# Preparing the next feed-forward batch one group sooner, with all weight sums on VectorE

## The reference

```python
def ternary_quant(w):
    scale = jnp.mean(jnp.abs(w)) + EPS
    q = jnp.clip(jnp.round(w / scale), -1.0, 1.0) * scale
    return w + jax.lax.stop_gradient(q - w)
...
up = jnp.einsum('bsd,ed->bse', x, wu)        # 512 -> 2048
gate = jnp.einsum('bsd,ed->bse', x, wg)      # 512 -> 2048
hidden = jax.nn.silu(up) * gate
return jnp.einsum('bse,de->bsd', hidden, wd) # 2048 -> 512
```

## Time and profile before

| | |
|---|---|
| Median of 3 runs | 760.04 us (760.04 to 761.48) |
| The profiled execution: its own time, and its span from first to last instruction | 760.04 us, 758.1 us |
| Busy share of the span: TensorE matmul, VectorE, ScalarE, GpSimd | 92%, 66%, 39%, 33% |
| TensorE clock granted, mean, as a share of 2.4 GHz | 0.973 |
| First product of the feed-forward part | 404.58 us |

### The profile page before, as it was taken

How to read it: one execution, slowest core, us unless ns; L and a number is a source line. 1 busy time by engine, 2 the same in 40 slices (tenths; PEclk the granted TensorE clock), 3 DMA queues, 4 the chain that set the end, 5 groups by cost and what they waited for, 6 DMA issues and landing times.

```text
span 758.1 us, 12681 instructions
## 1 busy us (share of the span) xinstructions
PE 695.5 (92%) x4745; PEld 457.6 (60%) x4776; DVE 503.4 (66%) x814; ACT 295.2 (39%) x450; POOL 250.6 (33%) x242
## 2 busy tenths in 40 slices
PE   7999999999998799999889999499977999499995
PEld 5565456556564656665447777377755777377772
DVE  5566766766757565567756978388773978457664
ACT  4365554554545244443322433234332343123330
POOL 4204523333334600003640343435431543414222
PEclk9999999999999999999999999899997999899998
DMA  8924035036046587601220030202111120201001
GB/s 246 338 81 142 1 128 206 0 125 208 1 155 234 166 326 253 243 29 42 50 50 1 1 51 1 49 1 81 25 26 25 52 54 1 50 1 56 1 1 55
DMA packets 57910, 67.37 MB, mean 89 GB/s; under 512 B 35072, under 2 KB 35072, under 8 KB 56832
## 3 DMA queue, kind: packets, MB, share of 16 engines
q1 hardware_dynamic: 54016, 54.03, 23.5%
q0 software_dynamic: 3840, 12.59, 4.4%
HBM read 46.69 MB, written 12.59 MB: 78 GB/s over the span
## 4 chain that ended last, share of the span: by engine, by line
PE 74%; DVE 9%; issue 7%; ACT 4%; DMA 2%; SPq 1%; POOL 1%; another core or an unknown queue 0%; POOLq 0%; DVEq 0%; ACTq 0%
PE bank L1211 26%; PE bank L1482 25%; PE bank L1491 13%; PE bank L1204 4%; PE bank L1404 2%; DVE region L829 2%; PE bank L1368 2%; PE bank L1382 2%; DMA w_att<-stage 2%; DVE late L825 1%; DMA stage<-in_L_attn_Wv_dram 1%; ACT stage L639 1%; ACT stage L519 1%; DVE region L833 1%; ACT tmp L527 1%
## 5 line engine op out<-in xcount | busy, mean ns | idle before, releaser
L1482 PE MATMUL bank<-w_att,region 128*128 128x256 f16 x1024 | 130.9, 277 | 28.5 <-issue 28.5
L1482 PEld LDWEIGHTS bank<-w_att,region 128*128 128x128 bf16 x1024 | 101.6, 99 | 48.7 <-issue 29.9
L1491 PE MATMUL bank<-region,w_moe 128*128 128x512 bf16 x481 | 115.5, 383 | 3.9 <-DVE w_moe L1122 2.1
L1132 DVE TENSOR_TENSOR n<-bank,n 128x512 f32<-128x512 f32 x112 | 71.7, 685 | 55.8 <-PE bank L1482 54.2
L1211 PE MATMUL bank<-late,w_att 128*128 128x512 f16 x384 | 86.8, 382 | 2.0 <-DVE region L872 1.9
L445 POOL TENSOR_TENSOR w_moe<-tmp,w_moe 128x512 f16<-128x512 f32 x30 | 36.0, 1200 | 154.3 <-ACT w_moe L669 154.3
L1491 PEld LDWEIGHTS bank<-region,w_moe 128*128 128x128 f16 x512 | 50.5, 99 | 51.2 <-DVE w_moe L1122 2.6
L326 POOL TENSOR_SCALAR ve<-mv 128x1 f32<-128x1 f32 (+2 forms) x29 | 10.9, 377 | 198.4 <-DVE mv L709 198.3
L662 ACT ACTIVATE n<-n,qs 128x512 f32<-128x512 f32 x64 | 44.5, 718 | 71.8 <-DVE n L1132 71.3
L1482 PE MATMUL bank<-w_att,late 128*128 128x256 f16 x512 | 68.6, 279 | 0.0
L1211 PEld LDWEIGHTS bank<-late,w_att 128*128 128x128 f16 x384 | 37.4, 98 | 45.0 <-DVE region L872 2.7
(11 more groups left out here) (161 smaller groups left out, 1143.1 us busy)
## 6 DMA issues: line engine op xcount, KB each, us to landing
stage<-in_L_ffn_W_up_dram SPq DMA_DIRECT2D x8, 1024.0 KB
stage<-in_L_ffn_W_gate_dram SPq DMA_DIRECT2D x8, 1024.0 KB, 5.4
rows<-sorted_residual SPq DMA_DIRECT2D x4, 1026.0 KB, 8.6
stage<-in_ctx_dram SPq DMA_DIRECT2D x4, 1024.0 KB, 6.6
stage<-in_L_ffn_W_down_dram SPq DMA_DIRECT2D x4, 1024.0 KB
nrm<-in_L_ffn_W_down_dram SPq DMA_DIRECT2D x4, 1024.0 KB, 8.0
n<-sorted_tokens SPq DMA_DIRECT2D x16, 256.0 KB, 5.8
rows<-in_x_dram SPq DMA_DIRECT2D x1, 3072.0 KB, 18.6
```

The lines of the kernel that those rows point to most:

```text
L1132: dve.tensor_tensor(out, wk_ps[(14 * n + m) % 4][:, :], other, ALU.add).then_inc(s["up_add"], 1)
L1482: mm = pe.matmul(wk_ps[bank][:, q * H:(q + 1) * H], w[:, c + q, k * P:(k + 1) * P], x3S_part[slot][:, h, m, k], start=(h == 0 and k == 0), ...
L1491: mm = pe.matmul(ffy_ps[t][:, :], hid[:, u, h, q, (t % 2) * P:(t % 2 + 1) * P], tern[2][:, c + q], start=(begins and q == 0 and h == 0), s ...
```

## The change

For batches 1 to 3 the preparation moves one group sooner. Normalise, sums, `x3_hi` and `x3_lo` of k = 2b+2 now stand in t = 0, those of k = 2b+3 in t = 2; statistics and rsqrt of k = 2b+3 in t = 1, and those of k = 2b+4 in t = 3. Those of k = 2 stand in expert step 15. All eight weight sums are on VectorE, in expert steps 10, 11, 13, 16 and 17 (before: VectorE's four in steps 10, 12, 15 and 16). In the last group only, `downs_before(2)` stands behind the gate products and not between them.

```diff
--- before.py
+++ after.py
@@ -428,11 +428,6 @@
                 pool.wait_ge(s["x3_lo_in"], 16 * k)
             pool.tensor_tensor(x3h[:, 1], x3_flat[:, 0:7 * H], x3h[:, 0], ALU.subtract).then_inc(s["x3_lo"], 1)
 
-        def gate_sum(dst, a, b, op, n):
-            if n > 0:
-                pool.wait_ge(s["gate_sums"], n)
-            pool.tensor_tensor(dst, a, b, op).then_inc(s["gate_sums"], 1)
-
         def send_out(b):
             for t in range(T):
                 pool.wait_ge(s["out_made"], T * b + t + 1)
@@ -447,13 +442,9 @@
 
         third_rsqrt(0)
         third_rsqrt(1)
-        pool.wait_ge(s["unit_copy"], 12 * T)
-        gate_sum(S1[1], A21[1], A22[1], ALU.add, 0)
         x3_lo(0)
-        gate_sum(S3[1], A11[1], A21[1], ALU.subtract, 1)
-        gate_sum(S2[1], S1[1], A11[1], ALU.subtract, 2)
         x3_lo(1)
-        gate_sum(S4[1], A12[1], S2[1], ALU.subtract, 3)
+        third_rsqrt(2)
 
         def group(b, t):
             n = T * b + t
@@ -461,9 +452,9 @@
                 hid_lo(n, 0, 0, g11)
                 hid_lo(n, 1, 3, g22)
             if b + 1 < B and t % 2 == 0:
-                third_rsqrt(2 * b + 2 + t // 2)
-            if b + 1 < B and t % 2 == 1:
                 x3_lo(2 * b + 2 + t // 2)
+            if (b + 1 < B and t == 1) or (b + 2 < B and t == 3):
+                third_rsqrt(2 * b + 3 + t // 2)
             if n < NT - 1:
                 hid_lo(n, 2, 1, g21)
                 hid_lo(n, 3, 2, g12)
@@ -687,7 +678,7 @@
                 act.wait_ge(s["y_mm"], STEPS)
             act.activation(g22, wk_ps[(14 * n + 7) % 4][:, :], ACT.Copy).then_inc(s["gate_copy"], 1)
             hid_hi(n, 0, 0, g11)
-            if b + 1 < B and t % 2 == 1:
+            if b + 1 < B and t % 2 == 0:
                 x3_hi(2 * b + 2 + t // 2)
             hid_hi(n, 1, 3, g22)
             hid_hi(n, 2, 1, g21)
@@ -1063,10 +1054,13 @@
             dve.wait_ge(s["x3_sum"], 4 * k + 3)
             less(6, 1, 5)
 
-        def up_sum(dst, a, b, op, n):
+        def weight_sum(j, n):
+            done = "gate_sums" if j else "up_sums"
+            dst, a, b, op = ((S1, A21, A22, ALU.add), (S3, A11, A21, ALU.subtract), (S2, S1, A11, ALU.subtract),
+                             (S4, A12, S2, ALU.subtract))[n]
             if n > 0:
-                dve.wait_ge(s["up_sums"], n)
-            dve.tensor_tensor(dst, a, b, op).then_inc(s["up_sums"], 1)
+                dve.wait_ge(s[done], n)
+            dve.tensor_tensor(dst[j], a[j], b[j], op).then_inc(s[done], 1)
 
         def expert_step(i):
             if i == 0:
@@ -1091,13 +1085,20 @@
                 x3_stats(i - 8)
             if i == 10:
                 dve.wait_ge(s["unit_copy"], 12 * T)
-                up_sum(S1[0], A21[0], A22[0], ALU.add, 0)
-            if i == 12:
-                up_sum(S3[0], A11[0], A21[0], ALU.subtract, 1)
+                weight_sum(0, 0)
+            if i == 11:
+                weight_sum(1, 0)
+            if i == 13:
+                weight_sum(0, 1)
+                weight_sum(1, 1)
             if i == 15:
-                up_sum(S2[0], S1[0], A11[0], ALU.subtract, 2)
+                x3_stats(2)
             if i == 16:
-                up_sum(S4[0], A12[0], S2[0], ALU.subtract, 3)
+                weight_sum(0, 2)
+                weight_sum(1, 2)
+            if i == 17:
+                weight_sum(0, 3)
+                weight_sum(1, 3)
 
         xs_lo(0)
         for i in range(STEPS):
@@ -1125,7 +1126,8 @@
         def group(b, t):
             n = T * b + t
             ends = n == NT - 1
-            nxt = 2 * b + 2 + t // 2 if b + 1 < B else None
+            nxt = 2 * b + 2 + t // 2 if b + 1 < B and t % 2 == 0 else None
+            then = 2 * b + 3 + t // 2 if t == 1 and b + 1 < B or t == 3 and b + 2 < B else None
 
             def up_of(out, m, other):
                 dve.wait_ge(s["up_mm"], 7 * n + m + 1)
@@ -1146,7 +1148,7 @@
             up_of(u21, 3, u12)
             if t == 1 and b > 0:
                 finish(b - 1, (2, 3), (16 * b, 16 * b))
-            if nxt is not None and t % 2 == 1:
+            if nxt is not None:
                 x3_normalise(nxt)
             dve.wait_ge(s["up_add"], 7 * n + 3)
             up_of(u22, 4, u21)
@@ -1155,9 +1157,9 @@
             up_of(u21, 5, u21)
             dve.wait_ge(s["up_add"], 7 * n + 5)
             up_of(u12, 6, u12)
-            if nxt is not None and t % 2 == 0:
-                x3_stats(nxt)
-            if nxt is not None and t % 2 == 1:
+            if then is not None:
+                x3_stats(then)
+            if nxt is not None:
                 x3_sums(nxt)
             if n > 0:
                 dve.wait_ge(s["hid_lo"], 4 * n)
@@ -1545,10 +1547,13 @@
             gate(1, S2, 5)
             gate(2, A12, 1)
             gate(3, S3, 4)
-            downs_before(2)
+            if n < NT - 1:
+                downs_before(2)
             gate(4, S1, 3)
             gate(5, A22, 6)
             gate(6, S4, 2)
+            if n == NT - 1:
+                downs_before(2)
             downs_before(3)
 
         pe.wait_ge(s["up_sums"], 4)
```

## The result

The changed kernel takes **723.44 us** (median of 4 runs, 722.43 to 723.56), against 760.06 us for the kernel before on the same chip: a ratio of 0.9511 (0.9494 to 0.9527). The profiled execution took 723.56 us. The forecast was 725.4 us.

A forecast was written before the change was run, and what follows sets the result against it. TensorE was taken as the bound, 92% busy, its feed-forward idle time nearly all three waits (28.5 us) between batches. −34.5 + 2.1 − 1.0 − 1.25 = −34.65 us took 760.04 us to 725.4 us, range 721.7 to 730.5 us.

The forecast's parts named there:

- The passages: Three passages between batches: all three 9.5 us waits and the slow restarts behind them go, −34.5 us.
- Group 0: Short first group: `x3_lo` delays the third `hid_lo`, a new TensorE wait before group 1's second down quarter, +2.1 us.
- VectorE's lag: Group 0: a normalise before the last `up` adds makes VectorE, and so the second `hid_lo`, about 1.0 us later.
- The weight sums: Expert steps: all eight sums on VectorE, no 4.77 us sum any more; −1.0 us, bounds −2.5 and +2.5.
- The two sums of step 13: Two sums, 2.5 us, before step 14's multiplication, mostly covered by TensorE's 12 matmuls; 0.3 us taken as cost.
- the two waits of 1.3 us: TensorE's waits of 0.58 us for step 10's `h_lo` and 0.74 us at 373.10, both taken back.
- The last group: Last group: VectorE starts its last row of instructions sooner, −1.25 us, bounds −1.7 and 0.
- What was costed at nothing: Preparation work in steady groups, `send_out` behind `x3_lo`, and the sums of steps 11, 16 and 17: 0 us.
- The port: Rival: in even groups GpSimd's `x3_lo` holds up VectorE's `gated`, about 1 us at six places; 731 us, chance 0.12.
- A preparation still late: Rival: a link such as the rsqrt slips, one of three passage waits stays; 737 us, chance 0.04.
- The clock: Rival: TensorE's granted clock falls under some 330 us without a hole; 775 us with 100 us low, chance 0.02.
- No wait in group 0: Rival: the 2.1 us wait doesn't form, or the experts gain more (−2.0 us); 722.3 us, chance 0.14.

The follow-up runs named there:

- fill_holes: Kernel before, with 164 small matmuls of unused result on TensorE in each of the three waits between batches; 755.39 us, ratio 0.9925.
- late_lo0: Changed kernel, with `x3_lo` of group 0 alone placed behind the third `hid_lo` and not before it; 721.98 us, ratio 0.9482.
- sums_only: Kernel before, with all eight weight sums on VectorE as the only change; 760.79 us, ratio 0.9995.
- sums_fill: Kernel before, with all eight weight sums on VectorE and small unused matmuls filling the three waits between batches; 752.87 us, ratio 0.9902.
- one_load_lo0: Changed kernel with `first` loads a step sooner, group 0's `x3_lo` behind the third `hid_lo`, and `second` reusing `first`'s register; 714.46 us, ratio 0.9396.
- hoist: Changed kernel, with TensorE's two register loads for the next step's `first` issued behind the current `first`; 717.96 us, ratio 0.9428.
- prep_only: Kernel before, with the earlier preparation alone; GpSimd keeps its four weight sums and the last group its order; 729.25 us, ratio 0.9577.
- tail_only: Kernel before, with only the last group's down quarter moved behind the gate products; 758.95 us, ratio 0.9975.
- hoist_lo0: Changed kernel, with register loads for `first` a step sooner and group 0's `x3_lo` behind the third `hid_lo`; 716.74 us, ratio 0.9419.
- fill_tail: Kernel before, with 34 small matmuls of unused result on TensorE in its last wait of 2.10 us; 760.03 us, ratio 0.9989.

## Why the prediction was right

**The passages** (−34.5 us). Right in size and in both pieces: −34.45 us between the same two moments of the traces, and `fill_holes` shows that 5.5 us of it were slow restarts (5.96 in the sum), the rest the waits. The working behind it set the lateness of 9.5 us against the 19.13 us by which the chain moves. In the changed kernel the last transpose of the next batch is over by 468.1 us (the last slice with DMA traffic of the stretch 460 to 478), and TensorE begins the batch at 477.8: at least 9.7 us of air, where 9.6 were worked out.

**Group 0** (+2.1 us). The place, the engine and the cause were right; the size came to +1.71 us between the two moments, 1.41 of it the wait itself. The mis-sized piece is VectorE's lag: worked out as 1.0 us, it is 0.6 at the second `hid_lo`. From the first feed-forward product to the start of that `hid_lo` it takes 421.60 − 404.58 = 17.02 us before and 421.54 − 403.89 = 17.65 us after. `late_lo0` shows that hardly anything else held up TensorE there: with `x3_lo` out of the way the same stretch takes 22.80 us, 0.14 more than before.

**The weight sums** (−1.0 us). The sign was right, the gain too small: −1.84 us in the changed kernel, 1.7 in `sums_only`, about the same by `sums_fill`. The two sums of step 13 were the part in doubt. VectorE's timeline, and TensorE behind it:

```profile
374.84 2.35 DVE L1063 TENSOR_TENSOR region<-region 128x2048 bf16<-128x2048 bf16 x2
```

```profile
379.38 2.76 PE L1213 MATMUL bank<-w_moe,w_att 128*128 x12 [0.56 <-issue]
```

Two sums take 2.35 us, and no sum takes 4.77 us any more. What each step gave can be read from the starts of the `first` products, before and after:

| from `first` of step | to that of step | before, us | after, us | difference |
|---|---|---|---|---|
| 11 | 12 | 7.12 | 6.05 | −1.07 |
| 12 | 13 | 7.32 | 7.70 | +0.38 |
| 13 | 14 | 7.17 | 6.20 | −0.97 |
| 14 | 15 | 6.41 | 6.78 | +0.37 |
| 15 | 16 | 7.50 | 6.81 | −0.69 |

The other steps of the stretch differ by 0.14 us together. The two sums of step 13 cost 0.37 us, where I had taken 0.3, and even that by way of the register loads: the `h_mul` behind them is late, and the loads wait for it. With the loads out of the way (`one_load_lo0`) neither `first` of step 15 nor the `second` after it waits. What was mis-sized is the gain. I had won back the two waits of 1.3 us; the two steps that had them are 2.04 us shorter. The rest, +0.38 and −0.69, is at the `first` of steps 13 and 16, which wait for "issue" in both kernels (1.10 and 1.47 us before, 1.49 and 1.02 after); `hoist` shows that these are register loads, which the prediction did not look at. The Trainium skill, SBUF — State Buffer, on the shared port pair, has such a sum wait for the whole of GpSimd's. `prep_only` agrees once more: VectorE's sum, begun at 389.35, ends at 393.05, 1.09 us behind the end of GpSimd's (391.96), and a sum alone takes 1.2 us; so it ran once GpSimd's was over.

**The last group** (−1.25 us). This is the term that was mis-sized most: −2.97 us. The schedule part was right: from the gate products to the start of the last run of down products it is 12.70 us before and 11.36 after, −1.34. The step that failed is that the term left the clock out. The kernel before ran its last matmuls in 7.90 us, part of them at a clock of 0.50, and the changed one in 6.22. I had read the lower clock behind the waits of 9.5 us, and did not look at the windows behind the 2.10 us wait. In the median it is worth less than in that profile, since the clock seems not to fall there each time: `tail_only` gives −2.0 us.

**What was costed at nothing** mostly held: apart from the `x3_lo` of group 0, no preparation step in the feed-forward part shows up as a wait of TensorE. The total owes something to luck: the stretch before expert step 9 took 1.15 us longer, with nothing changed in it, and so hid a part of what the other terms had too small (0.84, 0.39 and 1.72 us). The range has a slip: its own bounds add up to 730.8 and 721.8 us, not 730.5 and 721.7. Nothing hangs on it.

**The rivals.** *The port*: no wait of a microsecond in an odd group but the one in group 1, and `late_lo0` has none at all, with the `x3_lo` of the later even groups in their place. Where VectorE's `gated` and the `x3_lo` of group 2 meet, `gated` takes 1.64 us from 459.22 in place of 0.74, and `x3_lo`, begun after it at 460.28, takes 4.04 us, where one at 425.92 in `late_lo0` takes 3.60: both lose a little, and `gated` is not held for 4 us. *A preparation still late*: none. *The clock*: 1.00 from 404 to 716 us. *No wait in group 0*: there was one. But that rival's other half, experts that gain more, is what came: −1.84 us against the −2.0 that it assumed.

The parts run singly give −31.7, −0.1 and −2.0 us, 33.8 in all; the change gives 36.6. The rest is in two places that the runs show: the expert stretch of `prep_only` with its weight sum of 3.70 us, 1.05 us longer than before, and the weight sums' 1.7 us, which `sums_only` lost in its longer restarts.

## What to carry to other kernels

A wait in front of a batch costs its length and then the slow products behind it; read both, and read the granted clock behind every wait of a microsecond or two, at the end of the kernel too. When a preparation moves, work out how late it is and how much earlier it gets, then look at the first, shorter group, where its place in an engine's order can put it in front of something that is wanted sooner. Waits that the profile calls "issue" in front of products with a dynamic address may be register loads: issue them a step ahead, and load a value once. And compare one stretch over all traces that share its code: that priced the weight sums, where two times of whole kernels could not.

## What the runs showed of the hardware that was not expected

- **Register loads on TensorE.** Issued in front of the product that needs them, they show as 0.16 to 0.34 us of idle time at eleven of the 19 `first` of the changed kernel, 0.56 us at step 15, behind a late `h_mul`, and 1.02 and 1.49 us at steps 16 and 13, where DMA transposes were running (until about 366.2 us at step 13). A pair of them took up to 1.6 us from the end of the `h_mul` in front of it. Issued a step ahead they cost nothing at `first`; a load left in front of `second` still waited 0.67 us at 365.65, and with it gone that wait is gone as well. `hoist` and `one_load_lo0` together took 7.3 us off (8.5 less the 1.2 between `hoist` and `hoist_lo0`, which ran on two chips), 2.3 of it by dropping the second load. Why a load is slower beside transposes is open. The Trainium skill, DMA: Bandwidth & Descriptors, Latency and other measured facts, gives a `tensor_load` a floor of some 600 ns. The 1.6 us for a pair don't speak against that; no run here timed one by itself.
- **The clock after a short wait.** A wait of 2.10 us was followed by a granted clock of 0.50 in three of five profiles, waits of 0.43 to 0.77 us in none of nine, with the same matmuls behind them. What decides among the five is open; all three with the fall keep GpSimd's weight sums, and the two without have the sums on VectorE, but `before` and `sums_only` do the same work at the end.
- **Restarts behind the same wait.** After 9.5 us the same four products took from 4.98 to 5.98 us in three kernels (`before`, `tail_only`, `fill_tail`), growing from the first passage to the third in each, and 6.26 to 6.40 us in `sums_only`, which doesn't differ from them there. Why is open.
